# Attention's small products in two halves of 64 rows, with larger transfers and o turned in another bank

## What is computed

```
fq = jax.nn.elu(q) + 1.0
fk = jax.nn.elu(k) + 1.0
kv = jnp.einsum('bhnd,bhne->bnde', fk, v)        # per token n: 16 x 16, summed over heads h
qkv = jnp.einsum('bhnd,bnde->bhne', fq, kv)
k_sum = fk.sum(axis=1)
qk = jnp.einsum('bhnd,bnd->bhn', fq, k_sum)
attn = qkv / (qk[..., None] + 1e-06)
attn = attn.transpose(0, 2, 1, 3).reshape(b, n, c)
attn = attn @ wo + bo
x = q_x + attn
h = _ln(x, ln2_w, ln2_b)
h = jax.nn.gelu(h @ fc_w + fc_b, approximate=False)
return x + (h @ proj_w + proj_b)
```

## Time and profile before

| | |
|---|---|
| median of 3 runs | 728.25 us (727.19 to 729.0) |
| span of the profiled execution | 726.3 us |
| PE busy | 670.9 us, 92% |
| DVE, ACT, POOL busy | 481.1, 420.1, 326.5 us |
| instructions on PE | 6214 matmul records, 6214 weight loads |
| middle block, steps with attention alone | about 162 to 240 us |
| middle block, attention and hidden layer together | about 240 to 530 us |

### The profile page before, as it was taken

The page is one execution under the profiler, slowest core; times in us unless marked ns, Lnnn a source line. Parts: engine busy times, 40 slices in busy tenths (PEclk is TensorE's granted clock), DMA queues, the critical chain, the costliest instruction groups (busy, mean ns, idle before and its releaser), DMA issues.

```text
span 726.3 us, 17454 instructions
## 1 busy us (share of the span) xinstructions
PE 670.9 (92%) x6214; PEld 567.6 (78%) x6214; DVE 481.1 (66%) x1332; ACT 420.1 (58%) x841; POOL 326.5 (45%) x493
## 2 busy tenths in 40 slices
PE   7689999998777999999999999999999885999994
PEld 5449999975566788888888888888888663999994
DVE  7856757425688766767777768677676565777751
ACT  5755556502334767676767676766754642766660
POOL 5234563122232453545573664745547563353312
PEclk9879999999999999999999999999999998999998
DMA  8479788404656444544555555555433343567720
GB/s 264 149 241 322 229 270 276 139 29 119 98 99 109 91 66 90 95 87 66 101 86 85 117 84 129 68 108 91 86 73 96 116 132 109 167 215 217 219 93 29
DMA packets 287104, 95.56 MB, mean 132 GB/s; under 512 B 213989, under 2 KB 284737, under 8 KB 287019
## 3 DMA queue, kind: packets, MB, share of 16 engines
q1 hardware_dynamic: 272298, 85.48, 48.9%
q0 software_dynamic: 3840, 8.32, 3.6%
q10 hardware_dynamic: 10880, 0.66, 1.0%
HBM read 65.09 MB, written 29.40 MB: 130 GB/s over the span
## 4 chain that ended last, share of the span: by engine, by line
PE 75%; DVE 8%; issue 6%; ACT 4%; POOL 2%; DMA 2%; SPq 1%; ACTq 1%; POOLq 0%; DVEq 0%
PE bank L1735 68%; PE bank L1744 7%; DMA qkv_rows<-feats 1%; POOL hids L795 1%; SPq L373 1%; ACTq L373 1%; ACT hids L1038 1%; DMA x_all<-in_L_attn_q_x_dram 1%; ACT feats L1001 1%; POOL table L677 1%; ACT feats L999 0%; DVE kv_ L1679 0%; ACT ots L1063 0%; DVE sth L1687 0%; DVE att_ L1576 0%
## 5 line engine op out<-in xcount | busy, mean ns | idle before, releaser
L1735 PE MATMUL bank<-down_w,hids 128*128 128x256 f32 x768 | 105.8, 286 | 1.9 <-POOL hids L795 1.6
L1735 PE MATMUL bank<-hnts,up_w 128*128 128x512 f32 x384 | 104.4, 407 | 0.0
L795 POOL TENSOR_TENSOR hids<-hid,hids 128x512 fp32r<-128x512 f32 x64 | 83.1, 1298 | 41.0 <-ACT hids L1038 40.6
L1735 PEld LDWEIGHTS bank<-down_w,hids 128*128 128x128 f32 x768 | 95.7, 188 | 6.2 <-POOL hids L795 3.4
L1735 PE MATMUL bank<-qkv_w,xnts 128*128 128x256 f32 (+1 forms) x384 | 76.4, 346 | 5.7 <-DVE xnts L1589 4.8
L1735 PEld LDWEIGHTS bank<-hnts,up_w 128*128 128x128 f32 x384 | 67.5, 189 | 11.4
L1735 PEld LDWEIGHTS bank<-qkv_w,xnts 128*128 128x128 f32 x384 | 60.6, 189 | 18.2 <-DVE xnts L1589 7.5
L1035 ACT ACTIVATE hid<-bank,cols 128x512 f32<-128x512 f32 x64 | 44.1, 688 | 45.8 <-PE bank L1735 45.5
L786 POOL TENSOR_SCALAR sth<-sth 128x1 f32<-128x1 f32 x32 | 7.2, 226 | 125.3 <-DVE sth L1601 125.3
L1735 PE MATMUL bank<-a_w,xa_h 128*128 128x256 f32 x256 | 60.2, 379 | 0.0
L1735 PE MATMUL bank<-xa_xt,a_w 128*128 128x256 f32 x384 | 55.1, 294 | 1.4 <-DVE xa_xt L1327 1.4
(11 more groups left out here) (272 smaller groups left out, 1546.9 us busy)
## 6 DMA issues: line engine op xcount, KB each, us to landing
qkv_rows<-feats SPq DMA_DIRECT2D x32, 384.0 KB, 3.4
a_raw<-in_L_ffn_w_dram SPq DMA_DIRECT2D x32, 256.0 KB, 4.1
a_w<-in_L_ffn_w_dram SPq DMA_DIRECT2D x32, 256.0 KB, 3.7
b_raw<-in_L_ffn_w_dram SPq DMA_DIRECT2D x32, 256.0 KB, 3.2
b_w<-in_L_ffn_w_dram SPq DMA_DIRECT2D x32, 256.0 KB, 3.0
mid_rows<-x_all SPq DMA_DIRECT2D x8, 512.0 KB, 2.9
x<-mid_rows SPq DMA_DIRECT2D x32, 128.0 KB, 2.4
values<-qkv_rows SPq DMA_DIRECT2D x32, 128.0 KB, 2.9
```

The lines of the kernel that those rows point to most:

```text
L795: pool.tensor_tensor(hids[1][u % 3][:], hid[u % 2][:], f32(hids[0][u % 3][:]), ALU.subtract).then_inc(s_hidl, 1)
L1735: return pe.matmul(dst, left, right, start=start, stop=stop, skip_group_check=True)
```

## The change

Each set's grid is cut into two halves of 64 rows. A half holds four tokens, and its grid is 64 rows by 64 columns. Token `8s + 2u + r` of a tile lies in half `r` at rows `4k + u` (k is the head or the feature), columns `16u` on. A half's product has 64 rows and 64 columns, 32 weight columns as before, and there are 32 of them for each sum where there were 16. The halves write two banks: half 0 `B_ATT`, half 1 `B_KV`, each 256 columns wide. `u` is now what a transfer fetches: four each for values, keys and queries, each over 32 partitions, so 12 a tile.

ACT's `copy_kvt` and DVE's `attended` read the two banks with a pattern that puts the columns back in order. `B_KV` no longer takes the turned o: it goes to `B_TURN`, which zn had, and the two uses of `B_KV` by the second router go to `B_V`. The waits on those banks move with them. The tensors keep their places through a filler tile.

The diff, cut to its core:

```diff
-            keys = tiles(mid, "keys_", 2, [P, SETS, P])
-            queries = tiles(mid, "queries_", 2, [P, SETS, P])
+            keys = tiles(mid, "keys_", 2, [P, SETS, HALF])
+            queries = tiles(mid, "queries_", 2, [P, SETS, HALF])
+            tile(mid, "below_x", [P, 2, SETS, P])
...
+        sums = banks[:, B_ATT:B_KV + 1, 0:4 * HALF]
...
         def keys_by_sp(n):
-            return (4 if n == 0 else 5) if n < HELPED else 8
+            return 2 if n < HELPED else QUADS
         def queries_by_sp(n):
-            return (2 if n == 0 else 6) if n < HELPED else 8
+            return (1 if n == 0 else 3) if n < HELPED else QUADS
...
+        def of_quad(c, n, u):
+            return qkv_rows[c, n * P:(n + 1) * P, :].rearrange("(s u r) (k x) -> u (r k) s x", u=QUADS, r=HALVES, k=16)[u]
+
+        def issue_values(engine, n, u):
+            engine.dma_start(values[n % 2][u::QUADS, :, 0:HD], of_quad(2, n, u)).then_inc(s_kvin[n % 2], 16)
+
+        def issue_keys(engine, n, u):
+            engine.dma_start(keys[n % 2][u::QUADS, :, u * HD:(u + 1) * HD], of_quad(1, n, u)).then_inc(s_kvin[n % 2], 16)
+
+        def issue_queries(engine, n, u):
+            engine.dma_start(queries[n % 2][u::QUADS, :, u * HEADS:(u + 1) * HEADS], of_quad(0, n, u)).then_inc(s_qin[n % 2], 16)
...
-                act.copy(kvt[:], bank[B_ATT][:].rearrange("p (i c) -> p i c", i=4)).then_inc(s_kvt, 1)
+                act.copy(kvt[:].rearrange("p i (r d u) -> p i r d u", r=HALVES, d=HD),
+                         sums.rearrange("p r (i u d) -> p i r d u", i=4, u=QUADS)).then_inc(s_kvt, 1)
...
-                dve.transpose(att[:], bank[B_ATT][:].rearrange("p (i t h) -> p h i t", i=4, t=8)).then_inc(s_att, 1)
+                dve.transpose(att[:], sums.rearrange("p r (t h) -> p h t r", h=HEADS)).then_inc(s_att, 1)
...
                 for i in range(4):
                     for j in range(4):
-                        last = mm(bank[B_ATT][32 * j:32 * j + 32, i * P:(i + 1) * P], values[n % 2][:, set_of(i, j)],
-                                  keys[n % 2][:, set_of(i, j)], True, True)
+                        for r in range(HALVES):
+                            rows = slice(r * HALF, (r + 1) * HALF)
+                            last = mm(sums[32 * j:32 * j + 32, r, i * HALF:(i + 1) * HALF],
+                                      values[n % 2][rows, set_of(i, j)], keys[n % 2][rows, set_of(i, j)], True, True)
...
-                        last = mm(bank[B_ATT][32 * j:32 * j + 32, i * P:(i + 1) * P], kv[:, i, 32 * j:32 * j + 32],
-                                  queries[n % 2][:, set_of(i, j)], True, True)
+                        for r in range(HALVES):
+                            rows = slice(r * HALF, (r + 1) * HALF)
+                            last = mm(sums[32 * j:32 * j + 32, r, i * HALF:(i + 1) * HALF],
+                                      kv[rows, i, 32 * j:32 * j + 32], queries[n % 2][rows, set_of(i, j)], True, True)
...
                 if at(s, 5) is not None:
-                    pe.wait_ge(*kv_free)
+                    pe.wait_ge(*turn_free)
                     turn_o(s - 5)
-                    kv_free = (s_ol, s - 4)
+                    turn_free = (s_ol, s - 4)
...
                 for n in turned_at(s, 1):
-                    pe.wait_ge(*kv_free)
-                    turned(n, bank[B_KV])
-                    kv_free = (s_bfeat, n + 1)
+                    pe.wait_ge(*v_free)
+                    turned(n, bank[B_V])
+                    v_free = (s_bfeat, n + 1)
```

More of the change, by code:

```diff
@@ L75, in f32 @@
             return ap.bitcast(F32)
-        bank = [ctx.enter_context(nc.psum_tensor(f"bank{i}", [P, 512], F32)) for i in range(8)]
+        banks = ctx.enter_context(nc.psum_tensor("bank", [P, 8, 512], F32))
+        bank = [banks[:, i] for i in range(8)]
         ident = tile(ctx, "ident", [P, P])
@@ L560, in load_keys @@
             def load_keys(n):
-                i, rows = n % 2, slice(n * P, (n + 1) * P)
+                i = n % 2
                 sp.wait_ge(s_grid[i], 16 * (n // 2 + 1))
@@ L566, in load_keys @@
                     sp.wait_ge(s_st1, n - 1)
[L567 to L570, removed]
+                for u in range(QUADS):
+                    issue_values(sp, n, u)
+                for u in range(keys_by_sp(n)):
+                    issue_keys(sp, n, u)
             def load_queries(n):
@@ L574, in load_queries @@
                     sp.wait_ge(s_st2, n - 1)
-                for t in range(queries_by_sp(n)):
-                    issue_queries(sp, n, t)
+                for u in range(queries_by_sp(n)):
+                    issue_queries(sp, n, u)
             def store_x2(g):
@@ L1008, in help_queries @@
                     act.wait_ge(s_st2, n - 1)
-                for t in range(queries_by_sp(n), 8):
-                    issue_queries(act, n, t)
+                for u in range(queries_by_sp(n), QUADS):
+                    issue_queries(act, n, u)
             def help_keys(n):
@@ L1017, in help_keys @@
                     act.wait_ge(s_st1, n - 1)
-                for t in range(keys_by_sp(n), 8):
-                    issue_keys(act, n, t)
+                for u in range(keys_by_sp(n), QUADS):
+                    issue_keys(act, n, u)
             def copy_kvt(n):
@@ L1089, in _ @@
                 for n in turned_at(s, 1):
-                    features(n, bank[B_KV])
+                    features(n, bank[B_V])
                 if 0 <= s - ATTENTION_OVER - 2 < PAIRS:
@@ L1630, in _ @@
                 if routed(s, 2) is not None and routed(s, 2) < NG - 2:
-                    read_counts(routed(s, 2), bank[B_KV])
+                    read_counts(routed(s, 2), bank[B_V])
                 if routed(s, 2) == NG - 2:
@@ L2017, in turn_o @@
                 for k in range(KD):
-                    last = turn(bank[B_KV][:, k * P:(k + 1) * P], on[n % 2][:, k * P:(k + 1) * P])
+                    last = turn(bank[B_TURN][:, k * P:(k + 1) * P], on[n % 2][:, k * P:(k + 1) * P])
                 last.then_inc(s_ot, 1)
```

32 lines of the change are left out of this document (10 added, 22 removed).

## The result

The changed kernel takes 730.25 us (median of 20 runs, 729.09 to 732.97), the kernel before 729.07 us in 20 runs beside it. The ratio is 1.0024, with an interval of 1.0016 to 1.0031. I had forecast 716.3 us, 12 us faster, with a range of 711.0 to 724.0; by the ratio it is 1.8 us slower, which is within the 0.3% that I had set as "the same". The profiled spans are 729.0 us after and 726.3 us before.

A forecast was written before the change was run, and what follows sets the result against it. PE was taken to bound the kernel from 240 to 530 us, a step's latencies from 162 to 240. The terms 7.2 + 5.0 - 1.0 + 0.5 + 0.3 = 12.0 us took 728.25 to 716.3 us, range 711.0 to 724.0.

The forecast's parts named there:

- Transfers: SP's and ACT's issues fall from 17 to 12; shifts of the early stores taken together as 0, 1 us either way.
- The turned o: Early steps 5 to 9: `turn_o` waits for zn's second half, about 0.2 us a step, 1.0 us lost.
- I take 0.30 us saved: Each sum on PE: 0.30 us saved of 1.01, with 0.43 us the best case.
- 0.005 us each ... 0.64 us at most: Instruction starts within a sum: 128 at 0.005 us each take 0.64 us at most, partly before the sum begins.
- the 7.2 of the sum: `sum_att` on PE: 24 of them at 0.30 us saved each, 7.2 us gained.
- `sum_kv`'s room: Before `project`, which waits for ACT's copy of v: room of 0.10 to 0.49 us lets 5.0 of 6.9 us through.
- last sign of being wrong: Full steps: the prediction is wrong if another wait than that for v fills PE's time.
- Copies: ACT's copy of `kvt` and DVE's transpose, reading two banks with a stride: 0 change for both.
- The second rival: ACT's strided copy of `kvt` takes 0.3 us longer and the room of `sum_kv` is gone: 722.6 us, chance 0.12.
- The 0.5 us gained by fewer issues of ACT at 227.78: Early chain: ACT has one issue fewer just before its relu, 0.5 us gained.
- The third: Eight groups don't work side by side, or halves of a column group take turns: 728.8 us, chance 0.07.
- The fourth: PE's instruction supply binds; at 0.028 us a pair each of 47 sums loses 0.78 us: 765 us, chance 0.08.

The follow-up runs named there:

- `before12`: Kernel before with only its transfers changed, 12 a tile for 17, so attention pairs wrong values; 731.41 us, ratio 1.0042.
- `kv_only`: Changed kernel with 17 transfers a tile and only `sum_kv` in halves, `sum_att` whole; 731.26 us, ratio 1.0029.
- `idle_o`: Changed kernel plus idle products where PE waited early, before `turn_kv` in step 4 and `turn_o` in steps 6 to 9; 726.71 us, ratio 0.9979.
- `att_kv`: Changed kernel with 17 transfers, only `sum_att` in halves, and `turn_o` at its old place in `B_KV`; 724.53 us, ratio 0.9948.
- `att_only`: Changed kernel with 17 transfers a tile and only `sum_att` in halves, `sum_kv` whole; 726.97 us, ratio 0.9981.
- `no_idle`: Kernel before without its idle products in the steps of attention; 727.91 us, ratio 0.9991.
- `r_outer`: Changed kernel with early idle products, both sums doing all products of the upper 64 rows, then all of the lower; single run, 733.95 us.
- `full_early`: Changed kernel with early `turn_o` in an idle bank, ACT's helping key issues later, one key issue from SP to ACT, 4 idle products; 725.24 us, ratio 0.9948.
- `t17`: Changed kernel with the 17 transfers a tile of the kernel before; 730.71 us, ratio 1.0009.

## Why the prediction was wrong, step by step

Two steps failed in the early steps: "Transfers", taken as 0, costs 1.6 to 2.6 us (`before12` at the seventh tile and by its median), and "The turned o", taken as 1.0 us of waits, also lets the clock fall, for 2 to 3.4 us that no term held. In the full steps the mechanism was right and the sizes were not: 5.0 us for 12.2.

- **One sum.** The step "I take 0.30 us saved" gave 0.22. The mechanism was right: four rounds at 0.056 us, half of the 0.109 that a stream of 128 columns took. I had bounded the supply of instructions by "0.005 us each ... 0.64 us at most", and taken too little of it: the last 32 pairs come at 0.010 us a pair. `sum_att` is worth 24 x 0.22 = 5.3 us for the 7.2 of the sum.
- **`sum_kv`'s room.** Forecast: 5.0 of 6.9. `kv_only` shows 2.7 of 5.0. The rooms at `project` are as the step had them (0.05, 0.11, 0.16, 0.49 us left in the changed kernel), but `project` is not the only follower: DVE's read of the v bank in the routing steps took 0.9 us that the step did not look for. And 2.7 is from the fastest execution of `kv_only`.
- **Both sums together.** Between the 8th and the 30th `sum_kv` the changed kernel is 4.1 us shorter than the kernel before, 0.19 us a step where the forecast had 0.5. Its 44 sums should give 9.7 us; they give 8.1, since some stall (last section). And 3.8 come back: 1.6 ahead of the transposes of `hn` (in part a wait for ACT's copy at line 858, 0.8 us in all), 0.7 between `qkv` and `down_mid` (the wait for DVE), 0.6 ahead of `project`, 0.6 at the logits and 0.5 ahead of `down_mid` in the routing steps. The forecast looked at the wait for v alone. Its own last sign of being wrong came true: PE's waits of over 0.15 us from 240 to 530 us went from 2.0 to 4.0 us, and only 0.9 of them are for v.
- **Copies.** Forecast 0, measured 0: ACT's copy of `kvt` takes 586 ns, DVE's transpose 706. The second rival falls.
- **The turned o.** "About 0.2 us, in the five steps" is what shows where the clock holds: in `idle_o` the `sum_att` of the second, third and fourth tile stand 2.38, 2.59 and 2.80 us behind, 0.2 more each. But the step priced a wait, and not what the wait does to the clock. `att_kv` against `att_only` shows 2.5 us for the wait and the clock together.
- **Transfers.** "I take these together as 0, with 1 us either way": this step failed. It counted issues, 12 for 17, at the 0.45 us of one of keys. But an issue of 32 rows takes 0.63 us, and v's single one (0.37 us) became four of them, all ahead of the next tile's store. No row of before showed an issue of the new form, and the step put no bounds around it. `before12` measures 2.6 us, with one fall of the clock in it. The 0.5 us gained by fewer issues of ACT at 227.78 came in `before12` (0.6 us there), but as much in `att_kv` and `no_idle`, which issue as the kernel before does: that long issue in before's trace was no property of the kernel.
- **The clock.** It is in no term of the sum, and it costs 3.3 us early by the two ratios, 2.1 to 3.4 by the traces. The forecast even read the early steps as bound by latencies and PE as busy 62.55 of 78.00 us there, and then moved `turn_o` to where it joined two idle times. The earlier trace rows gave a clock of 0.98 for that stretch, and I took it as given.
- **Rivals.** None of the five is what happened. The third names almost the measured time, 728.8, but that is luck: its mechanism is refuted by `r_outer` and by the 0.79 us of a sum. The fourth has the right cause in a mild form: the supply of instructions does bound the second half of a sum, at 0.010 us a pair and not at 0.028. The 25 ns between starts of the Trainium skill, quoted in the prediction, are contradicted again: pairs of one round start 0.007 us apart.

In sum, for the traces: 0.5 us ahead of the change's reach, 5.7 us lost early, 5.0 gained in the full steps, 0.15 between 547 and 609 us and 1.3 at 609 us make the 2.7 us between the spans. The 1.3 at 609 us stay unexplained.

## What to carry to other kernels

Price what a change does where latencies bind as carefully as what it does where the engine is full: there a wait can cost the clock, and the clock costs more than the wait. Take the price of a transfer's issue from a row of its own form, or bound it from both sides; a smaller number of issues is not less time. And where two parts of a change belong together, measure each alone: half of this one, `sum_att` in halves with the transfers and `turn_o` as before, gives 0.5% where the whole gives nothing.

## What the runs showed of the hardware

- Sixty-four pairs (32 products) of 64 rows and 32 weight columns run in eight groups at once into two banks; a round of eight with 64 columns takes 0.056 us. The first 32 pairs start within 0.25 us, 0.007 us from pair to pair in a round; the others follow at about 0.010.
- Changing the shape cost about 0.1 us at the one kind of place that shows it. In the kernel before the 16 pairs of the logits (128 rows, 32 columns) run into `sum_kv` of the same shape; from the first logits' pair to the sum it is 0.46 us there (the earlier trace rows shows the same kind of edge behind a sum), and 0.57 us where the sum has 64 rows.
- Where both sums are in halves, single sums stall. One of the kernel after:

```profile
384.89 0.74 PE L1742 MATMUL bank<-keys,values 64*32 64x64 f32 x50
385.95 0.34 PE L1742 MATMUL bank<-keys,values 64*32 64x64 f32 x14 [0.33 <-issue]
```

  It waits for nothing that the profile shows. Eleven of the 64 sums of the kernel after take over 0.67 us from first to last, up to 1.19 (one of them, at 187.77 us, at the low clock); in the kernels with one sum in halves none does. The long stalls come back at the same sums: the `sum_kv` of the sixth tile has one in six of the seven kernels with both sums in halves, of 0.29 to 1.27 us between two of its pairs (not in `full_early`), that of the 19th tile in the kernel after and in `full_early`. The instructions that PE's program fetches grew too (the first queue of kind "instruction" has 50 packets before, 58 with one sum in halves, 66 with both). That stalls keep their place in the program would fit a fetch, but that the fetch is the cause was not tried; it stays open.
- An issue on SP took 0.45 us for 16 rows and 0.63 for 32, each of 16 pieces of 64 bytes a row; those are medians. Single ones took up to 3.0 us: from 250 to 528 us 38 of the 361 issues of keys and queries of the kernel before took over 1 us, and 48 of the 357 of `t17`.
